# Fourier-operator tower: the half inverse stored and loaded two quads at a time, with four slots for mode weights

## What is computed

```python
v = concat([x, gx, gy]) @ p_w + p_b                       # 64 images, 32 channels
for i in range(4):
    x_ft = rfft2(v)
    out_ft[:, :, :12, :12]  = einsum('bixy,ioxy->boxy', x_ft[:, :, :12, :12],  W1[i])
    out_ft[:, :, -12:, :12] = einsum('bixy,ioxy->boxy', x_ft[:, :, -12:, :12], W2[i])
    v = irfft2(out_ft) + einsum('bcxy,cd->bdxy', v, w_w[i]) + w_b[i]
    v = (v - mean(v)) * rsqrt(var(v) + eps) * bn_g[i] + bn_b[i]
    if i < 3: v = relu(v)
h = v @ q_w + q_b                                         # 64 x 64 tokens of 64
# then a class token, one linear-attention block and one mixture of 8 experts
```

## Time and profile before

| what | value |
|---|---|
| median of 3 runs | 1614.44 us (1611.79 to 1614.73) |
| the profiled execution | 1609.92 us, span 1608.1 us |
| PE / DVE / ACT / POOL busy | 1274.0 / 822.2 / 524.0 / 274.3 us |
| mean granted TensorE clock | 0.880 |
| queue of SP | 182522 packets, 291.19 MB |
| half-inverse loads (L1024) | 96 transfers of 384 KB, median 9.4 us to landing |
| half-inverse stores (L977) | 66 transfers of 512 KB, median 7.1 us to landing; 6 of 384 KB, 6 of 128 KB |
| weight loads (L1103) | 48 transfers of 384 KB, median 5.8 us to landing |

### The profile page before, as it was taken

How to read it: one execution, slowest core, us unless ns; L and a number is a source line. 1 busy time by engine, 2 the same in 40 slices (tenths; PEclk the granted TensorE clock), 3 DMA queues, 4 the chain that set the end, 5 groups by cost and what they waited for, 6 DMA issues and landing times.

```text
span 1608.1 us, 40075 instructions
## 1 busy us (share of the span) xinstructions
PE 1274.0 (79%) x18115; PEld 749.9 (47%) x18115; DVE 822.2 (51%) x886; ACT 524.0 (33%) x770; POOL 274.3 (17%) x376
## 2 busy tenths in 40 slices
PE   3489489999968759999896975999989777952587
PEld 3354155555545325555553532554555454312562
DVE  6432257777633226766663322666756522019745
ACT  1133234444433314443442321344444422000140
POOL 5541300220214300202021421001202040200000
PEclk9789779999979779999997986999999988985788
DMA  5469987988529999999971898989999052970001
GB/s 138 102 169 277 238 188 190 223 214 191 139 43 234 284 206 318 294 365 309 283 240 35 220 275 208 302 287 319 308 305 304 14 194 108 368 242 8 1 1 27
DMA packets 196820, 328.52 MB, mean 204 GB/s; under 512 B 35544, under 2 KB 141416, under 8 KB 177700
## 3 DMA queue, kind: packets, MB, share of 16 engines
q1 hardware_dynamic: 182522, 291.19, 63.3%
q0 software_dynamic: 14128, 34.76, 8.5%
HBM read 164.38 MB, written 142.64 MB: 191 GB/s over the span
## 4 chain that ended last, share of the span: by engine, by line
PE 57%; DMA 16%; DVE 10%; SPq 8%; ACT 5%; issue 3%; POOL 0%; DVEq 0%; ACTq 0%; POOLq 0%
PE ps L1439 13%; PE ps L1475 11%; PE ps L1507 7%; PE ps L1495 6%; PE ps L1370 4%; SPq L986 3%; DMA arena<-mixed_modes 3%; PE ps L1464 3%; PE ps L1400 3%; PE ps L1379 2%; DMA maps<-arena 2%; DMA mixed_modes<-arena 2%; PE ps L1455 2%; DMA inputs<-maps 2%; DMA inputs<-mixed_modes 1%
## 5 line engine op out<-in xcount | busy, mean ns | idle before, releaser
L1475 PEld LDWEIGHTS ps<-arena 48*128 48x128 f32 x3072 | 191.5, 198 | 120.5 <-issue 83.7
L1475 PE MATMUL ps<-arena 48*128 48x128 f32 x3072 | 211.4, 290 | 40.6 <-DMA arena<-half_inverse 33.3
L931 POOL DMA_DIRECT2D arena<-arena x162 | 95.6, 599 | 819.0 <-ACT arena L1280 818.3
L1263 ACT ACTIVATE arena<-ps,arena 128x1024 f32<-128x1024 f32 x96 | 112.2, 1202 | 248.6 <-PE ps L1475 207.5
L1370 PE MATMUL ps<-arena 64*64 64x64 f32 x2304 | 145.6, 285 | 49.4 <-DMA arena<-arena 49.4
L1370 PEld LDWEIGHTS ps<-arena 64*64 64x64 f32 x2304 | 130.9, 155 | 110.3 <-issue 104.9
L1272 ACT ACTIVATE ps<-ps 128x1024 f32<-128x1024 f32 x144 | 145.5, 1011 | 107.0 <-PE ps L1439 106.8
L1799 DVE STREAM_TRANSPOSE arena<-ps 128x1024 f32<-128x1024 f32 x96 | 177.1, 1928 | 3.5 <-PE ps L1495 3.5
L1439 PE MATMUL ps<-arena 32*32 32x512 f32 x2944 | 159.0, 621 | 5.3 <-issue 4.3
L1507 PE MATMUL ps<-arena 128*64 128x96 f32 x2304 | 129.0, 265 | 38.6 <-DVE arena L1799 30.5
L1507 PEld LDWEIGHTS ps<-arena 128*64 128x64 f32 x2304 | 109.1, 147 | 98.1 <-issue 57.3
(11 more groups left out here) (295 smaller groups left out, 1308.7 us busy)
## 6 DMA issues: line engine op xcount, KB each, us to landing
arena<-half_inverse SPq DMA_DIRECT2D x96, 384.0 KB, 9.4
half_inverse<-arena SPq DMA_DIRECT2D x66, 512.0 KB, 7.1
maps<-arena SPq DMA_DIRECT2D x112, 256.0 KB, 4.0
maps<-inputs SPq DMA_DIRECT2D x112, 256.0 KB, 6.4
arena<-maps SPq DMA_DIRECT2D x28, 1024.0 KB, 10.4
maps<-arena SPq DMA_DIRECT2D x28, 1024.0 KB, 6.3
inputs<-maps SPq DMA_DIRECT2D x28, 1024.0 KB, 9.2
arena<-in_mode_w POOLq DMA_DIRECT2D x48, 384.0 KB, 5.8
```

What stands on the lines that cost most here:

```text
L1263: nc.scalar.activation(half(h_out(l, q), h)[:, 1024 * pair:1024 * pair + 1024], ps[:, 2 * pair:2 * pair + 2, :].rearrange("p b n -> p (b n ...
L1475: last = nc.tensor.matmul(ps[:, b, at:at + 128], gtile[s][rows, 4 * b + 2 * h + n, :], iy[rows, :], start=False, stop=(i >= 2 and n == 1))
```

## The change

The DRAM tensor of the half inverse now keeps two neighbouring quads side by side. A store of one ky writes 8 rows of 256 floats (1 KB) per partition and half, in place of 16 rows of 128 floats (512 B). One load brings two quads, 48 partitions x 16 KB, into one tile of twice the size; the tile of a pair is chosen by the parity of the pair. All four `xhalf` tiles now lie on the two `gtile` tiles and none on `turned`. The SBUF for this comes from the ring of mode weights, which has four slots in place of six. Some tiles of the last stage get other addresses.

```diff
-RING = 6
+RING = 4
-    half_d = dram("half_inverse", [2, QUADS, KY, 4, 16, QUAD * CHANNELS])
+    half_d = dram("half_inverse", [2, QUADS // 2, KY, 4, 16, 2 * QUAD * CHANNELS])
-        A_YT = A_G + 2 * 2048
+        A_YT = A_G + 2 * 4096
-        xhalf = [view(at, 2048) for at in (A_G, A_G + 2048, A_P, A_P + 2048)]
-        gtile = [t.rearrange("p (x n) -> p x n", x=16) for t in xhalf[0:2]]
+        xhalf = [view(A_G + 2048 * s, 2048) for s in range(4)]
+        gtile = [view(A_G + 4096 * s, 4096).rearrange("p (x n) -> p x n", x=16) for s in range(2)]
...
         def slot_use(l, q):
-            return QUADS // 2 * l + q // 2
+            return QUADS // 4 * l + q // 4
...
-                    sp.dma_start(half_d[t, a // 128:b // 128, ky].rearrange("q r g n -> (r g) q n"),
-                                 xhalf[ky % 4][64 * t:64 * t + 64, a:b].rearrange("p (q n) -> p q n", n=128))\
+                    sp.dma_start(half_d[t, a // 256:b // 256, ky].rearrange("q r g n -> (r g) q n"),
+                                 xhalf[ky % 4][64 * t:64 * t + 64, a:b].rearrange("p (q n) -> p q n", n=256))\
...
-            def g_load(l, i):
-                q = ORDER[l][i]
+            def g_load(l, k):
                 for t in range(2):
-                    sp.dma_start(gtile[i % 2][64 * t:64 * t + 4 * KY],
-                                 half_d[t, q].rearrange("y r g n -> (y r) g n"))\
-                      .then_inc(g_in[i % 2], 16)
+                    sp.dma_start(gtile[k % 2][64 * t:64 * t + 4 * KY],
+                                 half_d[t, ORDER[l][2 * k] // 2].rearrange("y r g n -> (y r) g n"))\
+                      .then_inc(g_in[k % 2], 16)
...
                 g_load(l, 0)
+                store_columns(KY - 1, *((HEAD, 2048) if head(l)[0] == 0 else (0, 2048 - HEAD)), ix_st[3])
+                sp.wait_ge(ix_st[3], half_stored(l, KY - 1) + 32)
                 g_load(l, 1)
-                store_columns(KY - 1, *((HEAD, 2048) if head(l)[0] == 0 else (0, 2048 - HEAD)), ix_st[3])
...
-                sp.wait_ge(ix_st[3], half_stored(l, KY - 1) + 32)
                 for i in range(QUADS - KEPT):
...
-                    g_load(l, i + 2)
+                    if i % 2 and i < QUADS - 4:
+                        g_load(l, i // 2 + 2)
...
                 if h == 0:
-                    pe.wait_ge(g_in[s], 32 * (slot_use(l, q) + 1))
+                    pe.wait_ge(g_in[q // 2 % 2], 32 * (slot_use(l, q) + 1))
...
-                if q == 0 and h == 0:
-                    for ky in (KY - 2, KY - 1):
-                        dve.wait_ge(ix_st[ky % 4], half_stored(l, ky) + 32)
```

More of the change, by code:

```diff
@@ L151, in tower_kernel @@
         A_G = A_P + POSITIONS
-        A_YT = A_G + 2 * 2048
+        A_YT = A_G + 2 * 4096
         A_STAGE = A_YT + 2048
-        A_SMALL = 37200
+        A_SMALL = 39440
         assert A_STAGE + 8 * 576 <= A_SMALL
@@ L188, in tower_kernel @@
         packed = view(A_RING, 2560)
-        kx_last = view(A_RING + 2560, 768)
+        kx_last = view(A_STAGE + 1024, 768)
         x_last = view(A_RING, 768)
-        g_last = view(A_RING + 3328, 1024).rearrange("p (x b) -> p x b", x=16)
+        g_last = view(A_STAGE + 1792, 1024).rearrange("p (x b) -> p x b", x=16)
         lines = view(A_RING, 2048)
@@ L290, in tower_kernel @@
         b2p = [take(DIM // 2).bitcast(bf16) for _ in range(3)]
-        assert top[0] <= A_SMALL
+        assert top[0] <= A_STAGE + 1024
         top[0] = 0
@@ L1466, in out_set @@
                 if h == 0:
-                    pe.wait_ge(g_in[s], 32 * (slot_use(l, q) + 1))
+                    pe.wait_ge(g_in[q // 2 % 2], 32 * (slot_use(l, q) + 1))
+                quads = gtile[q // 2 % 2][:, :, 128 * s:128 * s + 128]
                 for i, turn in enumerate(TURNS):
@@ L1474, in out_set @@
                             at = 256 * n + 128 * half_x
-                            last = nc.tensor.matmul(ps[:, b, at:at + 128], gtile[s][rows, 4 * b + 2 * h + n, :],
+                            last = nc.tensor.matmul(ps[:, b, at:at + 128], quads[rows, 4 * b + 2 * h + n, :],
                                                     iy[rows, :], start=False, stop=(i >= 2 and n == 1))
```

## The result

The changed kernel is slower by 3%, far more than forecast: 1662.15 us (median of 4, 1656.63 to 1668.52) against 1614.59 us. The ratio is 1.030, with a 95% interval of 1.026 to 1.034. The profiled execution has a span of 1659.6 us, 51.5 us more than before.

A forecast was written before the change was run, and what follows sets the result against it. TensorE bounds the passes, a DRAM relay with nearly full DMA engines the mixing stages. Later pass starts +13.8 and faster stores -9.0 give +4.8 us on 1614.4: 1619 us, range 1606 to 1628; other terms count 0.

The forecast's parts named there:

- Part 4: Pair loads inside the passes, half as many bursts twice as long: cost 0, up to +10 us in two passes.
- the cover of the input loads: In the passes, 24 us of slack against 20.6 us to landing for input loads behind a burst; hidden with 3 us left.
- Rival 3: Stores gain nothing and bursts delay input loads in the passes: +13.8 plus up to 5 us, 1628 to 1633; chance 0.11.
- Part 1: First load of a pass has twice the bytes and lands 4.6 us later; three passes, +13.8 us.
- Part 2: Stores in 1 KB rows in the mixing stages gain 0.3 us each, ten per stage, three stages: -9.0 us.
- the 4.6 named as the limit: Mixing stages: the forecast counts as wrong if the gain per stage is over 4.6 us.
- the 321 GB/s row: Pass 1 traffic with rows of 2 and 8 KB, used to price stores: 3.27 us each against 3.76 for 512 B rows.
- rival 2: Store gain of 0.46 us each in the mixing stages, -13.8 us, cancels the later pass starts: 1614; chance 0.24.
- rival 1: Row length counts: each mixing-stage store gains 0.7 us or more, -21 us, in all -7 us: 1607; chance 0.24.
- Part 3: Waits for the last stores removed from VectorE's first transpose and moved in SP's queue at pass start: counted 0, bounds -3.0 and 0.
- Part 5: Four weight slots in the mixing stages only move load deadlines: cost 0, or +2 us per stage if landing took 5 us longer.
- the 3 us left: Stage at 471 us: weights of ky 4 negated by 487.9, TensorE takes it up at 491.13; tightest margin 3 us.

The follow-up runs named there:

- Experiment 7: Changed kernel without half-inverse loads inside the passes; only the first two pairs are loaded, later quads use stale data: 1584.32 us, ratio 0.9841.
- Experiment 1: Changed kernel with each pair load cut into rows of 8 KB, four transfers, the two partition halves in turn: 1620.74 us, ratio 1.006.
- experiment 5: Changed kernel with pair loads in rows of 8 KB, both transfers to partitions 0 to 47 first, then both to 64 to 111: 1644.33 us, ratio 1.019.
- experiment 6: Changed kernel with pair loads in rows of 4 KB, eight transfers, the two partition halves in turn: 1598.08 us, ratio 0.9915.
- experiment 12: Changed kernel with pair loads in rows of 4 KB, all four transfers to partitions 0 to 47 first, then four to 64 to 111: 1620.31 us, ratio 1.0018.
- Experiment 2: Changed kernel, rows of 16 KB kept, but one transfer (half the partitions) after each quad instead of two after every second: 1640.62 us, ratio 1.016.
- Experiment 9: Kernel with one-quad loads in 512 B pieces, up to four quads ahead, but stores and DRAM layout of the kernel before (512 B rows): 1616.36 us, ratio 1.0024.
- experiment 4: Changed kernel, its DRAM layout and 1 KB store rows kept, each load bringing one quad in 512 B pieces, four quads ahead: 1604.00 us, ratio 0.9949.
- experiment 3: Kernel before the change with four weight slots in place of six and nothing else: 1614.06 us against 1613.96, ratio 1.0016.

## Why the prediction was wrong

**Part 4 is the step that failed.** It priced pair loads in the pass at 0, with up to +10 us if the cover of the input loads gave way. They cost +53.5 us. The bursts were judged by who waits for the data of a transfer. That was right as far as it goes: input loads landed after 19.9 us at most in pass 1 and 19.5 in pass 2 (20.6 at most forecast), and nobody waited for them visibly. But the burst had another victim, by the traces: TensorE's own instructions, which come through the same 16 engines. "The bytes are the same" was taken for "the cost is the same". Experiment 7 shows that these loads make the whole loss of the passes. Experiments 1, 5, 6 and 12 show that two properties of the transfers do it, the length of the row (with the number of transfers) and the run onto one half of the partitions. Experiment 2 shows that the length of the burst adds to it. Rival 3 had the bursts as a cause, but through late input loads, and at +5 us. The DMA page of the Trainium skill (DMA: Bandwidth & Descriptors, "Back-pressure in remote DMA") says, of transfers from one core to another, that a saturated SBUF port stalls the engines that write to it, their other queues included. The loads here come from DRAM, which that section does not treat. The trace would fit the same mechanism, with no instruction packet in the 10.3 us from the load's issue at 366.73 to 377, but no run here isolates it. What holds the packet back stays open.

**Part 1 was right in kind and near in size.** +16.1 us measured in the three passes for +13.8; 12.1 us to landing where 11.5 to 12 was named as the sign. Each of the three starts cost 5.1 to 5.7 us, not 4.6.

**Part 2 was right in kind and sized too small.** Stores in rows of 1 KB gained 13.6 us in the profiles (9.0 forecast), which is 4.5 us per stage (5.7, 2.1 and 5.8), just under the 4.6 named as the limit. Over the ten stores of a stage that the prediction counts this is 0.45 us each, where 0.3 was chosen. Experiment 9 against 4 gives 0.42 us over all twelve. The value that the 321 GB/s row gave, 3.76 - 3.27 = 0.49, was nearer; rival 2 took 0.46 from the same row, and rival 1 took 0.7 for a midpoint that is 0.87. Of the two rules of the Trainium skill (DMA: Bandwidth & Descriptors) that the prediction named, experiment 9 speaks against the one of full line rate from 512 B on, for these stores. The one of about 3 cycles per packet, an estimate of 8% or 0.3 us, has the sign and less than the size.

**Part 3 was right as far as seen:** neither wait stands in the chain of the changed kernel at the start of pass 1, and what the removed ones gave is not to be told from the later start. **Part 5 was right:** experiment 3. TensorE's two waits for the negation in the middle mixing stage come to 2.5 us, so one of them is over the 1 us named. The longest landing of 8.7 us was read from the last mixing stage; in the stage that was priced it is 9.1, which takes 0.4 of the 3 us left.

Without the +53.5 us of the passes, the rest of the trace comes to -1.9 us where +4.8 was forecast. That is inside the range, but nearer to rival 2 than to the forecast. Experiment 1 is the changed kernel with the passes nearly restored, and its 1620.7 us are within 2 us of the predicted 1619. That is in part luck: in its trace the passes cost 4.9 us, the starts 13.4, and the stages gave 11.4.

## What to carry to other kernels

Judge a burst of DMA not only by who waits for its data. The instruction queue shares the engines. The sign to look for is a stop in the middle of a group of matmuls, marked "issue", that ends 1 to 2 us after a packet of the instruction queue. Where a load goes to part of the partitions on both sides of 64, as here (0 to 47 and 64 to 111), try rows of some KB that change sides often; 4 KB in turn gained 1.4% on the kernel before by itself. Making a transfer larger is a gain where its rows are short (512 B to 1 KB) and can be a loss where they are long already.

## What was not expected of the hardware

For the same 1.5 MB into 48 + 48 partitions with full or nearly full engines, one side after the other gave 166 GB/s in rows of 16 KB and 163 in rows of 4 KB, and rows of 4 KB in turn gave 195. A q8 packet came late enough to stop TensorE behind rows of 16 KB and not, in pass 0, behind rows of 4 KB at that same rate. Pieces of 512 B on the SBUF side (experiment 4) do not hold up the instructions: the passes are 269.1, 291.5 and 296.6 us. Where the waits are, the clock is lower too: in pass 0 of the changed kernel the granted clock is 0.91 in place of 0.94, and the same matmuls take 7.4 us longer. What stays open is why the instruction packet of pass 0 comes only when the first transfer of the pair has landed, and not after a few rows of it.
